# Second mixture of experts: all experts for two groups, tiles of chosen experts for six

## The reference

```python
logits = xf @ Wr + br                       # xf: 4096 tokens x 128, 8 experts
topk_w, topk_idx = jax.lax.top_k(logits, 2)
topk_w = softmax(topk_w)
gate = sum(one_hot(topk_idx, 8) * topk_w[..., None], axis=1)
h = relu(einsum('th,ehf->etf', xf, W1) + b1[:, None, :])   # 128 -> 256
y = einsum('etf,efh->eth', h, W2) + b2[:, None, :]         # 256 -> 128
out = einsum('te,eth->th', gate, y)         # x = x + 0.5 * out
```

## Time and profile before

| | before |
|---|---|
| median of 3 runs | 1617.76 us (1615.98 to 1620.47) |
| the profiled execution, its own time | 1617.13 us |
| its span | 1615.4 us |
| busy share PE / DVE / ACT / POOL | 87% / 62% / 54% / 26% |
| mean granted clock of TensorE | 0.946 |

### The profile page before, as it was taken

How to read it: one execution, slowest core, us unless ns; L and a number is a source line. 1 busy time by engine, 2 the same in 40 slices (tenths; PEclk the granted TensorE clock), 3 DMA queues, 4 the chain that set the end, 5 groups by cost and what they waited for, 6 DMA issues and landing times. The chain is left out here.

```text
span 1615.4 us, 37203 instructions
## 1 busy us (share of the span) xinstructions
PE 1412.7 (87%) x11945; PEld 980.0 (61%) x11945; DVE 1005.8 (62%) x3167; ACT 878.3 (54%) x1559; POOL 424.8 (26%) x709
## 2 busy tenths in 40 slices
PE   2688888888769999997899969999799997999998
...
POOL 4355565565310000111233322323222220000000
...
DMA packets 62787, 102.97 MB, mean 64 GB/s; under 512 B 7942, under 2 KB 51934, under 8 KB 53470
## 3 DMA queue, kind: packets, MB, share of 16 engines
...
## 5 line engine op out<-in xcount | busy, mean ns | idle before, releaser
L1126 ACT ACTIVATE e_buf<-ps_q 128x1024 f32<-128x1024 f32 x192 | 196.2, 1022 | 113.8 <-PE ps_q L1741 113.8
L1633 PEld LDWEIGHTS ps_o<-w,e_buf 128*128 128x128 f32 x2048 | 241.5, 192 | 23.1 <-issue 21.0
L1633 PE MATMUL ps_o<-w,e_buf 128*128 128x128 f32 x2048 | 250.6, 276 | 0.0
L2306 DVE SCALAR_TENSOR_TENSOR e_buf<-ps_o,gate,e_buf 128x128 f32<-128x128 f32 x512 | 144.0, 344 | 121.7 <-PE ps_o L1633 120.1
L1752 PE MATMUL ps_o<-e_buf,v_st 128*32 128x256 f32 x3072 | 208.8, 390 | 0.2
L1126 ACT ACTIVATE e_buf<-ps_k 128x1024 f32<-128x1024 f32 x192 | 195.5, 1018 | 13.8 <-PE ps_k L1741 12.0
L1062 ACT ACTIVATE e_buf<-ps_q,b_t 128x512 f32<-128x512 f32 x128 | 87.6, 686 | 147.7 <-PE ps_q L1625 145.9
L2047 DVE TENSOR_REDUCE mx<-ps_q 128x6 f32<-128x768 f32 x128 | 121.8, 952 | 64.8 <-PE ps_q L1340 63.8
L1062 ACT ACTIVATE e_buf<-ps_k,b_t 128x512 f32<-128x512 f32 x128 | 87.2, 687 | 131.7 <-PE ps_k L1625 130.0
L2520 DVE COPY o_sb<-ps_o 128x256 f32<-128x256 f32 x192 | 81.0, 422 | 107.8 <-PE ps_o L1752 64.8
L1741 PE MATMUL ps_q<-q_st,k_st 73*128 73x256 bf16 x768 | 121.4, 282 | 30.3 <-DMA q_st<-scr_q 18.2
(11 more groups left out here) (323 smaller groups left out, 2644.4 us busy)
## 6 DMA issues: line engine op xcount, KB each, us to landing
...
k_st<-scr_k SPq DMA_DIRECT2D x192, 192.0 KB
...
```

The source lines that it names most:

```text
L1126: act.activation(e_buf[g % 2][:, hp * 2 % HG:hp * 2 % HG + 2, :], (ps_q, ps_k)[hp % 2][:, :, :], ACT.Exp).then_inc(sem("fast_exp"), 1)
L1633: last = mm(ps_o[:, e % 2, t * P:(t + 1) * P], h_sb[e % 2][:, f, t * P:(t + 1) * P], w2[:, e * NF + f, :], start=f == 0, stop=f == NF - 1)
L2306: last = stt(acc[u][:, t, :], ps_o[:, e % 2, t * P:(t + 1) * P], gate[u][:, t, e:e + 1], acc[u][:, t, :], ALU.mult, ALU.add)
```

## The change

Only the last stage computes something else. Groups 0 and 1 (DG = 2) still go through `mixture`. The other six are taken as NC = 3 blocks of two groups, 1024 tokens each. The 2048 (token, expert) pairs of a block are sorted by expert into tiles of 128 rows, each tile with one expert; 23 tiles (SLOTS) are always enough and always computed, in six "quads" of four, the last of three. For each block:

- DVE ranks the logits as before, with one more step (`sel`, the two chosen), and `slots` works out in 22 instructions each pair's row, each tile's expert and the two weights. PE's `positions` gives it the counts (16 products of bf16).
- POOL's `send` scatters the normed tokens to `slots_in` in DRAM with 16 indirect DMAs of 128 rows; SP loads quads of it back, PE transposes them, ACT copies them to `xt`.
- For each tile, PE, ACT and DVE each read the tile's expert with a `value_load`. DVE copies w1 of that expert to a ring of four (`tile_weights`), PE makes two hidden products (`tile_hidden`, three tiles ahead), ACT two Relus, PE one product with b2 in three bf16 parts and two with w2 (`tile_out`). DVE empties ps_o once a quad (`quad_out`), SP stores the quad to `slots_out`.
- POOL's `fetch` gathers the two results of each token with 16 more indirect DMAs a block, DVE's `collect` adds them with their weights to x.

The router work (norm, logits, ranks) of groups 2 to 5 lies in `more(g, e)`, called after each expert of groups 0 and 1, and that of groups 6 and 7 among the tiles of block 0. On PE `ahead` places tokens and logits of two groups in group 0, `positions(0)` after expert 1 of group 1, two more transposes and one logits there. ACT's relu bank and exponentials follow the same places. Elsewhere: some semaphores are merged; POOL makes the bf16 parts of b2, and SP zeroes `slots_in` (three DMAs of 1.6 MB), both beside the first mixture.

```diff
+CB = 4
+CT = CB * NT
+DG = 2
+ND = NG + DG
+NC = (NG - DG) // 2
+SLOTS = 2 * CT + EXP - 1
+QT = 4
+QUADS = (SLOTS + QT - 1) // QT
...
+            sp.wait_ge(sem("consts"), CONSTS + 7)
+            for j in range(3):
+                sp.dma_start(scr_b[j].rearrange("(e c) -> e c", e=EXP), b2_parts[:, j, :]).then_inc(sem("stored"), 16)
+            for i in range(NC):
+                sp.dma_start(slots_in[i].rearrange("(i p) c -> p i c", p=P),
+                             blank.unsqueeze(1).broadcast_to([P, QUADS * QT, C])).then_inc(sem("stored"), 16)
...
+            def load_quad(c, q):
+                k = c * QUADS + q
+                if k >= 2:
+                    sp.wait_ge(sem("M_gt"), past("M_gt", k - 1))
+                n = in_quad(q)
+                sp.dma_start(xs[:, k % 2, 0:n, :],
+                             slots_in[c].rearrange("(q p t) c -> q p t c", p=P, t=QT)[q][:, 0:n, :])\
+                  .then_inc(sem(f"tile_in_{k % 2}"), 16)
+            def store_quad(c, q):
+                k = c * QUADS + q
+                sp.wait_ge(sem("M_comb"), past("M_comb", k + 1))
+                sp.dma_start(slots_out[c].rearrange("(q p t) c -> q p t c", p=P, t=QT)[q], ys[:, k % 2, :, :]).then_inc(sem(f"tile_out_{k % 2}"), 16)
...
+            results(0)
+            sp.dma_start(b2_rows, scr_b.rearrange("j (e c) -> j e c", e=EXP)).then_inc(sem("window_in"), 16)
+            results(1)
+            sent(0)
+            load_quad(0, 0)
+            load_quad(0, 1)
+            for c in range(NC):
+                for q in range(QUADS):
+                    if q + 2 < QUADS:
+                        load_quad(c, q + 2)
+                    elif c + 1 < NC:
+                        if q + 2 == QUADS:
+                            sent(c + 1)
+                        load_quad(c + 1, q + 2 - QUADS)
+                    store_quad(c, q)
+                    if c == 2 and q == 4:
+                        results(DG)
+                        results(DG + 1)
+            for g in range(DG + 2, NG):
+                results(g)
...
+            def send(c):
+                pool.wait_ge(sem("D_slots"), c * 2 + 2)
+                if c == 0:
+                    pool.wait_ge(sem("stored"), 16 * (NC + 3))
+                for t in range(CT):
+                    for k in range(2):
+                        pool.indirect_dma_start(
+                            slots_in[c], bass.IndirectOffsetOnAxis(ap=slot_no[c][:, k, t:t + 1], axis=0),
+                            normed_rows(DG + c * 2 + t // GT)[:, t % GT, :], None).then_inc(sem(f"sent_{c % 2}"), 16)
+            def fetch(c, w):
+                j = c * (CT // 2) + w
+                if w == 0:
+                    for i in range(2):
+                        pool.wait_ge(sem(f"tile_out_{i}"), (c + 1) * QUADS // 2 * 16)
+                if c:
+                    pool.wait_ge(sem("M_gate"), past("M_gate", (j - CT // 2 + 1) * 2))
+                for t in range(2 * w, 2 * w + 2):
+                    for k in range(2):
+                        pool.indirect_dma_start(
+                            y_back[:, t, k, :], None, slots_out[c],
+                            bass.IndirectOffsetOnAxis(ap=slot_no[c][:, k, t:t + 1], axis=0))\
+                            .then_inc(sem(f"back_{w}"), 16)
+            for c in range(NC):
+                send(c)
+            for c in range(NC):
+                for w in range(CT // 2):
+                    fetch(c, w)
...
+            def tile_relu(c, i):
+                j = c * SLOTS + i
+                e = act.value_load(expert[c][0:1, i:i + 1], min_val=0, max_val=EXP - 1)
+                act.wait_ge(sem("M_h"), past("M_h", j + 1))
+                for f in range(NF):
+                    last = act.activation(h_chan[:, j % 4, f, :], tile_bank(j)[:, f * P:(f + 1) * P],
+                                          ACT.Relu, bias=b1_t[:, bass.ds(e * NF + f, 1)])
+                last.then_inc(sem("M_relu"), 1)
...
-            mixture_groups(pe, lambda g, u: mixture(g, u, NG, False))
...
+            def quad_rows(c, q):
+                k = c * QUADS + q
+                pe.wait_ge(sem(f"tile_in_{k % 2}"), (k // 2 + 1) * 16)
+                if k:
+                    pe.wait_ge(sem("M_gtc"), past("M_gtc", k))
+                else:
+                    pe.wait_ge(sem("M_relu"), past("M_relu", 0))
+                for t in range(in_quad(q)):
+                    last = tr(ps_k[:, 1, t * P:(t + 1) * P], xs[:, k % 2, t, :])
+                last.then_inc(sem("M_gt"), 1)
...
+            def tile_owner(c, i):
+                return pe.value_load(expert[c][0:1, i:i + 1], min_val=0, max_val=EXP - 1)
+            def tile_hidden(c, i):
+                j, k, t = c * SLOTS + i, c * QUADS + i // QT, i % QT
+                pe.wait_ge(sem("M_relu"), past("M_relu", max(j - 3, 0)))
+                if t == 0:
+                    pe.wait_ge(sem("M_gtc"), past("M_gtc", k + 1))
+                pe.wait_ge(sem("M_acc"), past("M_acc", j + 1))
+                for f in range(NF):
+                    last = mm(tile_bank(j)[:, f * P:(f + 1) * P], w_now[:, j % 4, f * P:(f + 1) * P],
+                              xt[:, k % 2, t * P:(t + 1) * P], start=True, stop=True)
+                last.then_inc(sem("M_h"), 1)
+            def tile_out(c, i, e):
+                j, k, t = c * SLOTS + i, c * QUADS + i // QT, i % QT
+                if t == 0:
+                    pe.wait_ge(sem("M_comb"), past("M_comb", max(k - 1, 0)))
+                to = ps_o[:, k % 2, t * P:(t + 1) * P]
+                mm(to, ones_b[0:3, 0:P], b2_rows[:, bass.ds(e, 1), :].rearrange("p e c -> p (e c)"), start=True, stop=False)
+                pe.wait_ge(sem("M_relu"), past("M_relu", j + 1))
+                for f in range(NF):
+                    last = mm(to, h_chan[:, j % 4, f, :], w2[:, bass.ds(e * NF + f, 1), :].rearrange("p e c -> p (e c)"),
+                              start=False, stop=f == NF - 1)
+                if i % QT == in_quad(i // QT) - 1:
+                    last.then_inc(sem("M_out"), 1)
...
+            for c in range(NC):
+                for i in range(SLOTS):
+                    if i % QT == 0 and i // QT + 1 < QUADS:
+                        quad_rows(c, i // QT + 1)
+                    if i == SLOTS - 4 and c + 1 < NC:
+                        quad_rows(c + 1, 0)
+                    if i + 3 < SLOTS:
+                        at.append(tile_owner(c, i + 3))
+                        tile_hidden(c, i + 3)
+                    elif c + 1 < NC:
+                        if i + 3 == SLOTS:
+                            pe.wait_ge(sem("D_slots"), c * 2 + 3)
+                        at.append(tile_owner(c + 1, i + 3 - SLOTS))
+                        tile_hidden(c + 1, i + 3 - SLOTS)
+                    tile_out(c, i, at[c * SLOTS + i])
+                    if c == 0:
+                        if i == 0:
+                            mix_logits(ND + 3, 0)
+                        if i == 3:
+                            positions(1)
+                        if i == 7:
+                            mix_tokens(ND + 4)
+                        if i == 9:
+                            mix_logits(ND + 4, 0)
+                        if i == 11:
+                            mix_tokens(ND + 5)
+                        if i == 13:
+                            mix_logits(ND + 5, 0)
+                        if i == 15:
+                            positions(2)
...
-            mixture_groups(dve, lambda g, u: mixture(g, u, NG, False))
...
+            def slots(c):
+                s = Steps("M_step", past("M_step", c * (14 + SLOT_STEPS) + 14), SLOT_STEPS)
+                w = CT * EXP
+                dve.wait_ge(sem("M_lg"), past("M_lg", c * 3 + 3))
...
+            def tile_weights(c, i):
+                j = c * SLOTS + i
+                if i == 0:
+                    dve.wait_ge(sem("D_slots"), c * 2 + 1)
+                e = dve.value_load(expert[c][0:1, i:i + 1], min_val=0, max_val=EXP - 1)
+                if j >= 4:
+                    dve.wait_ge(sem("M_h"), past("M_h", j - 3))
+                dve.tensor_copy(w_now[:, j % 4, :], w1[:, bass.ds(e, 1), :].rearrange("p e f -> p (e f)"))\
+                    .then_inc(sem("M_acc"), 1)
+            def quad_out(c, q):
+                k = c * QUADS + q
+                n = in_quad(q) * P
+                dve.wait_ge(sem("M_out"), past("M_out", k + 1))
+                if k >= 2:
+                    dve.wait_ge(sem(f"tile_out_{k % 2}"), k // 2 * 16)
+                dve.tensor_copy(ys[:, k % 2, 0:in_quad(q), :].rearrange("p t c -> p (t c)"), ps_o[:, k % 2, 0:n])\
+                    .then_inc(sem("M_comb"), 1)
+            def collect(c, w):
+                j = c * (CT // 2) + w
+                dve.wait_ge(sem(f"back_{w}"), c * 64 + 64)
+                for k in range(2):
+                    for t in range(2 * w, 2 * w + 2):
+                        row = of_group(DG + c * 2 + t // GT)(t % GT)
```

(67 more changed lines are left out.)

372 lines of the change are left out of this document (323 added, 49 removed).

## The result

The change takes 1608.4 us (median of 14 runs, 1599.6 to 1616.4) against 1619.4 before (14 runs, 1611.1 to 1628.2): a ratio of 0.9927 with a 95% interval of 0.9910 to 0.9944. It is faster, by 11 us or 0.7%, where I forecast 36 us. The profiled execution took 1608.7 us with a span of 1607.0; my sum had 1579 for that span. So 28 us are to be found.

A forecast was written before the change was run, and what follows sets the result against it. The prediction took PE's count of products to bound the stage. Tiles start at 1441, blocks end at 1490, 1519 and 1551, the tail at 1579; plus 1.7 makes 1581, forecast 1582 us, range 1550 to 1625.

The forecast's parts named there:

- Begin of the second mixture: Start of the last stage: stays at 1360.8, the added zeros and b2 parts being hidden beside the first mixture.
- Groups 0 and 1: First two groups of the second mixture: x written at 1400 and 1436.3, with 2 us charged for DVE's lumps.
- Start of the tiles: From x of group 1 at 1436.3 through write, load, transposes and copy to PE's first tile product at 1441.
- One tile: Each tile in the blocks: PE's queue sets 1.28 us, its engine's 0.66 us overlapping it; DVE's queue 0.88.
- queue and engine don't overlap: Rival for the tiles: PE 1.94 us a tile, DVE 1.30, giving 1621 us in all; chance 0.10.
- No more than the queue's: Tiles at half PE clock: engine time doubles to 1.3 us a tile, no more than the queue's time.
- Block 0: First tile block: DVE's summed work sets 51.6 us from 1437, to 1490; first to first of blocks 49 us.
- Block 1: Second tile block: PE's queue sets it, 23 x 1.28 = 29.4 us, to 1519.
- a thing I had named as what would prove me wrong: Start of block 1 or 2: PE waiting for the loaded quads would show the forecast wrong.
- Block 2: Third tile block: PE 29.4 us, DVE 27.6, nearly equal, so 2 us for collisions: to 1551.
- End: Tail after 1551: emptying, store, sixteen gathers of 18.4 us, landing, collect and result, to 1579.
- the indirect DMAs are dear: Rival on POOL's scatters and gathers: 2.5 us each instead of 1.15, giving 1670 us; chance 0.18.

The follow-up runs named there:

- e9_slots: On top of e2_loads: block 0's second ranks, positions and slots one expert earlier on PE, DVE and ACT; ratio 0.9902 to the kernel before, mixture 236.6 us.
- e2_loads: The change with the first two loads of slot rows ahead of the store of group 1's result on SP; ratio 0.9915 to the kernel before.
- e3_no_owner: The change without PE's register loads of the tile's expert (always expert 0; DVE and ACT keep theirs); ratio 0.9924 to the kernel before.
- e1_logits: The change with the fourth chosen group's logits (PE) and the third's exponentials (ACT) ahead of the tiles; ratio 0.9874 to the kernel before.
- e6_queue: On top of e1_logits: block 1's positions and slots two tiles earlier, ACT's exponentials earlier and norm logarithms later; ratio 0.9867 to the kernel before.
- e12_lagged: The change with only SP's order altered: each quad's load ahead of one earlier store, across blocks too; ratio 0.9904 to the kernel before.
- e4_half: The change with 8 instead of 16 gathers in the last block, stale rows used for the second expert; ratio 0.9858 to the kernel before.
- e13_outs: The change with earlier logits, loads and slots, eight-weight ring, lagged stores, retimed router work, plus earlier quad emptying and two later result stores; 1581.2 us, ratio 0.9793.

## Why the prediction was wrong

Direction, range and order of steps were right; the size was three times too large. By its own steps, from 1579 to 1607:

- **Begin of the second mixture, +5.1 us.** 1365.9 against 1360.8. The thirteen profiled kernels that share this code began it at 1354.5 to 1368.4, on average 1361.3. So most of this piece is scatter of the one execution. That the zeros and b2's parts cost nothing is not shown: no run left them out, and in all thirteen comparisons the median gained less (by 1.2 to 5.4 us, 2.9 on average) than the second mixture got shorter from its 254.6. In the first mixture, from group 0's write of x to group 7's, the thirteen took 246.6 to 248.5 us, and the kernel before 246.2. (POOL's first scatter waits for the zeros as well, not only SP, as I had written.)
- **Groups 0 and 1, right:** 39.0 and 36.2 against 39 and 36.3. e9_slots adds that the same router work one expert earlier makes the two 2.6 us shorter, so part of what I had charged as lumps is a matter of order.
- **Start of the tiles, +1.4.** 6.1 instead of 4.7 from x to the first product (my terms add up to 5.05; I rounded). The load took 3.1 us from its issue to the transposes, not 2.7, and the four transposes 1.1, not 0.45, at a granted clock of 0.51. `send(0)` ran from 1419.3 to 1439.6 and not from 1410 to 1428; behind SP's wait for x it would have been the next thing that held the load, which e2_loads and e9_slots show.
- **One tile: right number, wrong ground.** I had 1.28 for PE's queue and 0.66 for its engine, counting five products at 0.11. The 0.11 in the earlier trace rows is the price of a record: one float32 product is two records there too (what I called 16 products are 16 records of 8 products). Nine records at 0.14 make 1.25, and the queue lies beside it (e3_no_owner). The loads took 0.30 us, the short end of the earlier trace rows. The Trainium skill (DMA: Bandwidth & Descriptors, section on latency and other measured facts) has about 600 ns for such a load; the medians here are 302 and 307 ns. The step failed twice and the errors cancelled. The rival "queue and engine don't overlap" is excluded for PE by the same run. For DVE the trace speaks for it: a weight came every 0.76 us where nothing else held it, 0.47 without a wait and 0.29 of copy, not 0.88 of queue with the copy beside it. No run took DVE's loads away.
- **Half clock.** "No more than the queue's" came from the same miscount. At 0.50 a tile took 2.22 us, 1.0 more than at full speed, and in block 0 half clock cost 7.3 us by the estimate above: a term that I had put at nothing.
- **Block 0, +11.3 (60.3 against 49), and 4.3 before its first tile is out.** This is the step that failed. I summed DVE's work and took for granted that it runs without a gap. From the filling of the pipe to the end of the block DVE stood 14.7 us for PE's logits and positions, which PE issues behind tiles whose weights stand behind that wait; PE in turn stood 16.0 us of the 60.3. e1_logits and e6_queue took 11.7 us out by order alone, 8.9 of it PE's standing and 2.2 its half clock. That they ended at 48.6, next to my 49, is in part luck: 27 weights at 0.76 and not 0.88 are 3 us less DVE work than I had summed, and in both runs one set of ranks (3 us) had moved ahead of the block. 4.3 is the cold filling of the pipe (1447.24 to 1451.58), which I had not priced.
- **Block 1, +5.0 (34.0 against 29).** Up to 2.1 is the load behind the store (e12_lagged), a thing I had named as what would prove me wrong, and not priced. The rest is the transposes of six quads on an engine that I held to be free: 6 x 0.43 = 2.6.
- **Block 2, -3.6 (28.4 against 32).** No collisions: DVE, busy 14.1 of 28.4 us, waited for no gather, and the last three tiles have no hidden products beside them (0.80 us each).
- **End, +4.8 (32.8 against 28).** My terms add up to 28.5, of which I took 28. Sixteen gathers at 1.25 are 20.0, not 18.4 (e4_half gives 1.2 to 1.4 each). From the last product to the first gather it was 5.0 us (1574.2 to 1579.15), not 3.2, and from the end of the last sum to the end of the span 5.3 (1601.7 to 1607.0), not 3.5. The last gather's rows were there 1.2 us after its 1.25, not 2.3.

The sum: 5.1 - 0.2 + 1.4 + 17.0 + 4.8 = 28.1, with 17.0 for the tiles (4.3 + 11.3 + 5.0 - 3.6).

The rival that the indirect DMAs are dear fell: 0.94 us busy and one each 1.25. Its mechanism did not show either. The Trainium skill (SBUF — State Buffer, sections on the two separate sides and on the bandwidth-pool intuition) says that a float32 copy within SBUF by DVE keeps POOL from writing descriptors. The 16 scatters of block 0 had no weight copy beside them, and the longest of all 48, 1203 ns, is the first of these; the 32 with copies beside them took 0.95 to 1.11 us. What shows is the other side: the 13 weight copies during which POOL's queue stood took 0.29 us each, and of the other 56, in the stretches in which POOL worked, 17 took 0.34 to 0.53. No run here took the copies away.

The forecast mixture was 218.2 us long (1360.8 to 1579), and e13_outs, with the same work in another order, takes 218.0. That is mostly chance: groups 0 and 1 and the pause came out 5.1 us below my terms, blocks 0 and 1 with the filling 4.9 above them. What the sum left out is the order in the queues and PE's half clock.

Left open: what PE's clock would give in block 0 if the pauses were gone altogether, and whether a group with all experts, run last, would hide the 32 us of the end. Neither was tried.
